# The router's place in the last group of a fused Mamba and mixture-of-experts block, and two queues for its last loads

## The reference, cut to what matters

```python
h = _layernorm(x) * (1 + cb) + sb
out = _swiglu(h, shared_gate_up, shared_down)
logits = einsum('bsd,ed->bse', h, gate_weight)
probs = softmax(logits)
top_p, sel = top_k(probs, 2)
top_p = top_p / (sum(top_p) + 1e-08)
for e in range(8):
    out = out + cw[..., e:e+1] * _swiglu(h, experts_gate_up[e], experts_down[e])
x = x + gb * out
```

## Time and profile before

| what | value |
|---|---|
| median of 3 runs | 744.22 us |
| the profiled execution's own time | 742.37 us |
| its span | 740.6 us |
| mean granted TensorE clock | 0.94 |
| busy PE / DVE / ACT / POOL | 88% / 74% / 59% / 54% |
| last group's shared expert and router | about 362 to 388 us |
| expert tiles | 392 to 715 us |
| end: results, last loads, output | 715 to 740.6 us |

### The profile page before, as it was taken

How to read it: one execution, slowest core, us unless ns; L and a number is a source line. 1 busy time by engine, 2 the same in 40 slices (tenths; PEclk the granted TensorE clock), 3 DMA queues, 4 the chain that set the end, 5 groups by cost and what they waited for, 6 DMA issues and landing times.

```text
span 740.6 us, 12188 instructions
## 1 busy us (share of the span) xinstructions
PE 651.5 (88%) x3026; PEld 501.9 (68%) x3026; DVE 550.7 (74%) x1220; ACT 440.0 (59%) x804; POOL 397.0 (54%) x329
## 2 busy tenths in 40 slices
PE   4778989889998989878778999999999999999960
PEld 1555766667675667656556877877878878777840
DVE  5787988989798997987565776677776667666752
ACT  4647666685767668563444666666666666666640
POOL 2424564738456464826245847567439448472560
PEclk9688989999899999998889999999999999999995
DMA  8303111202112020211331324241320414211407
GB/s 260 78 1 102 50 50 37 64 28 75 39 57 57 29 57 28 82 32 65 108 129 44 114 78 150 66 145 52 122 72 30 157 40 122 99 49 65 135 30 232
DMA packets 47381, 59.83 MB, mean 81 GB/s; under 512 B 8756, under 2 KB 34856, under 8 KB 47360
## 3 DMA queue, kind: packets, MB, share of 16 engines
q1 hardware_dynamic: 41600, 46.91, 20.9%
q0 software_dynamic: 5760, 12.67, 4.9%
HBM read 40.01 MB, written 20.84 MB: 82 GB/s over the span
## 4 chain that ended last, share of the span: by engine, by line
PE 51%; DVE 30%; issue 10%; ACT 2%; DMA 2%; POOL 2%; DVEq 1%; SPq 1%; POOLq 0%; ACTq 0%
PE PS L671 48%; PE PS L674 4%; DVE al L1322 4%; DVE acc L1335 3%; DVE prod L1315 2%; DVE dB L1359 2%; DVE yT L1425 1%; DVE wd L1408 1%; DVE PS L1315 1%; DVE h L1447 1%; DMA yT<-result_dram 1%; DVE stats_a L1299 1%; DVE diag L1412 1%; DVE stats_b L1299 1%; DVE nx_b L1434 1%
## 5 line engine op out<-in xcount | busy, mean ns | idle before, releaser
L1034 ACT ACTIVATE sg<-PS 128x512 f32<-128x512 f32 x216 | 128.7, 597 | 131.9 <-PE PS L671 121.7
L671 PE MATMUL PS<-xh,w_lo 128*128 128x512 f32 x405 | 176.1, 435 | 13.2 <-DVE prod L1315 10.4
L1315 DVE TENSOR_TENSOR PS<-PS,sg 128x512 f32<-128x512 f32 (+1 forms) x160 | 111.3, 697 | 91.7 <-PE PS L671 60.6
L671 PE MATMUL PS<-xl,w_hi 128*128 128x512 f32 x405 | 163.8, 404 | 0.0
L671 PE MATMUL PS<-xh,w_hi 128*128 128x512 f32 x405 | 163.4, 404 | 0.0
L547 POOL DMA_INDIRECT sorted_dram<-h,slot x64 | 73.4, 1147 | 93.0 <-DVE slot L1524 66.9
L671 PEld LDWEIGHTS PS<-xh,w_lo 128*128 128x128 f32 x405 | 78.4, 194 | 46.1 <-DVE prod L1315 16.4
L609 POOL DMA_INDIRECT result_dram<-y_rows,aux_d x84 | 83.0, 989 | 37.5 <-issue 20.1
L1042 ACT CAST ah<-PS 128x512 fp32r<-128x512 f32 (+1 forms) x160 | 93.0, 581 | 15.4 <-DVE PS L1315 13.3
L671 PE MATMUL PS<-ah,w_lo 128*128 128x512 f32 x216 | 93.7, 434 | 8.1 <-ACT ah L1042 4.3
L1322 DVE TENSOR_TENSOR al<-PS,ah 128x512 fp32r<-128x512 f32 x140 | 95.7, 684 | 3.4
(11 more groups left out here) (199 smaller groups left out, 1153.1 us busy)
## 6 DMA issues: line engine op xcount, KB each, us to landing
xin<-sorted_dram SPq DMA_DIRECT2D x20, 516.0 KB
stage<-in_w_gu SPq DMA_DIRECT2D x18, 448.0 KB
sorted_dram<-pad SPq DMA_DIRECT2D x9, 516.0 KB
h<-mods_dram SPq DMA_DIRECT2D x32, 128.0 KB, 6.2
stage<-in_w_dn SPq DMA_DIRECT2D x9, 448.0 KB
tab<-mods_dram SPq DMA_DIRECT2D x8, 384.0 KB, 3.4
out<-X SPq DMA_DIRECT2D x8, 256.0 KB, 5.1
stage<-result_dram SPq DMA_DIRECT2D x6, 256.0 KB, 4.2
```

The source lines that it names most:

```text
L671: return nc.tensor.matmul(out, lhsT, rhs, start=start, stop=stop, **k)
L1034: A.activation(dst, src, ACT.Silu).then_inc(s["silu_done"], 1)
L1315: V.tensor_tensor(product_in(where, c)[0:n, :], bank("up", where, c)[0:n, :], sg[0:n, c % 3, :], ALU.mult).then_inc(s["prod_done"], 1)
```

## The change

It has two parts, in two different stretches.

In the last group: ACT runs `router_exp` ahead of silu 0, where it stood between silu 1 and high 0. DVE runs `weights` and `place` ahead of `product` 0, so that `low` 0 follows `product` 0. PE runs `count_picks` after `gate_up` of chunk 1, where it stood after chunk 2. At the end: SP asks for the even groups' last rows, and ACT, which waits for the same semaphore value, asks for the odd ones.

```diff
-            for g in range(G):
+            for g in range(0, G, 2):
                 sp.dma_start(fin[g], res[1, g]).then_inc(s[f"final_in{g}"], 16)
...
-                if c == 2:
+                if c == 1:
                     count_picks(G - 1, LAST_COUNTS)
...
             copy_h2(G - 1)
+            router_exp(G - 1)
             silu(G - 1, 0, WIDE)
             for c in range(FC):
                 if c + 1 < FC:
                     silu(G - 1, c + 1, WIDE)
-                if c == 0:
-                    router_exp(G - 1)
                 high(G - 1, c, WIDE)
             keep_result(G - 1, WIDE)
...
+            tiles, first = tiles_of(act, E - 1)
+            act.wait_ge(s["results_out"], 64 * (first + tiles + 2))
+            apart(act)
+            rows = result_dram.rearrange("(k g p j) d -> k g p (j d)", k=2, g=G, p=P)
+            for g in range(1, G, 2):
+                act.dma_start(fin[g], rows[1, g]).then_inc(s[f"final_in{g}"], 16)
...
             pick(g)
+            weights(g)
+            place(g, LAST_COUNTS)
             product(g, 0, WIDE)
-            weights(g)
             low(g, 0, WIDE)
-            place(g, LAST_COUNTS)
```

## The result

The changed kernel took 742.42 us (median of 13 runs, 739.87 to 743.5) beside 744.18 us for the kernel before (13 runs). The ratio is 0.9966, with a 95% interval of 0.9952 to 0.9979: faster by 2.5 us, between 1.6 and 3.6. The forecast was 742.6 us and faster. A second set of runs of the same changed kernel gave a ratio of 0.9961 (0.9946 to 0.9976). The profiled execution took 741.35 us, span 739.3.

A forecast was written before the change was run, and what follows sets the result against it. PE was taken to bound the tile stage, DVE's wait for ACT the last group, and full DMA engines the end. Gains of 1.2 and 0.4 us, with zero for the clock, took 744.22 to 742.6 us; range 741.1 to 744.3.

The forecast's parts named there:

- Part one: Last group: DVE's 2.14 us idle goes, product 1 starts earlier; gain 1.2 us, between -0.15 and 1.2.
- The early slots: Last group: slots ready some 3.1 us earlier, for POOL's sorted rows and SP's tile load; costed at nothing.
- The clock: PE's granted clock around its last-group restart: low stretch costs 1.7 us; taken as zero, between -1.7 and 1.7.
- Part two: The end: two queues asking for the last rows fill unfilled DMA stretches; gain 0.4 us, between -0.5 and 0.87.
- The sum: Whole kernel: 1.2 from the last group plus 0.4 from the end, 1.6 us off the median 744.22.
- the second (the clock): PE's restart in the last group: clock stays up or returns sooner, worth up to 1.7 us; chance 0.15.
- The first (the end gains nothing): The end: DMA engines are the limit, so a second queue wins nothing; 743.0 us; chance 0.24.
- third: PE's restart in the last group: the low clock lasts as long again; 744.3 us; chance 0.08.
- fourth: Last group: the counts come no earlier, so DVE waits for PE instead of ACT; 744.0 us; chance 0.04.
- fifth: PE from 374 us on: clock stays low until the shared expert is done; 748.8 us; chance 0.05.

The follow-up runs named there:

- e3: The changed kernel with PE counting the picks behind chunk 2's matmuls again, as before the change; ratio to the kernel before 0.9985.
- e9: The changed kernel with DVE's old order, its plan moved behind low 1, and nine useless PE matmuls in pauses around the first tile; 737.14 us, ratio 0.9914.
- e8: The kernel before with 12 useless matmuls in PE's pause ahead of down 1; the interval of its ratio holds 0.998 and 1.000.
- e11: The changed kernel with ACT's exponential put back behind silu 1, DVE's new order kept; ratio to the kernel before 0.9971.
- e10: The kernel before with nine useless matmuls in PE's three pauses around the first tile; ratio to the kernel before 0.9972.
- e2: The kernel before with only the end's change, SP and ACT each asking for half of the last rows; ratio 0.9995.
- e1: The changed kernel with SP asking for all eight last rows and ACT for none; ratio to the kernel before 0.9967.

## Why the prediction was right, and where it was not

**Part one** was right in each step. The counts begin at 367.01, which is 4.26 us behind `take_logits` (4.32 in the prediction), DVE waits 0.33 for them (0.25 in the prediction) and 0.65 for high 0 (0.7), PE stands 1.71 us ahead of down 0 (1.7). Product 1 is 1.19 us earlier for 1.2, and gated 1.16. e3 shows that this hangs on the counts: with them behind chunk 2 the gain is -0.14 at gated, where the lower bound was -0.15. Two details were off. I put ACT's first table load behind the wait, and it runs ahead of it. It changed nothing here. And ACT was late in the kernel before not because it did two silus, which take 0.6 us each, but mainly because the second of them waited for its gate product until 366.12:

```profile
366.12 0.60 ACT L1034 ACTIVATE sg<-PS 128x512 f32<-128x512 f32 x1 [1.74 <-PE PS L671]
```

The exponential no longer stands behind that wait.

**The early slots** were costed at nothing, and nothing waited for them in the changed kernel. With a start 4.4 us earlier than the kernel before, in e9, PE does wait for the first tile's load.

**The clock** was the weak step, in what it looked at. The prediction took zero, between -1.7 and 1.7, and looked for it only behind PE's restart. There it was right: gated moved by as much as product 1, since the low stretch costs about the same before and after (the 38th matmul at 10.35 and 10.39 us behind the restart). The price of 1.7 us holds as well: at full clock the same matmul comes at 8.8 (e8, e11). But the kernel before has a second low stretch in the first tile, and the changed kernel has none, though PE makes pauses of the same kind there (0.77, 0.83 and 1.14 us). The prediction put nothing for that. Four profiles with a low stretch there have 18.33 to 18.77 us for that tile, the nine without it 16.75 to 17.92, and the means are 1.4 us apart. Against the four at full clock without a late step it is 1.6 to 2.0. e10 isolates it. Why the changed kernel falls on the good side stays open: e2 and e11, 0.14 us apart at gated, fall on different sides. The changed kernel did so in both of its profiles, so it isn't chance from one execution to the next, but nothing in the plan of the change aimed at it.

**Part two** came out larger in the profiles than its bounds: 0.4 us in the sum, between -0.5 and 0.87, and 1.2 us between the means of the spans, or about 1.0 with the 0.2 us lost outside them. Counted from the first issue, the changed kernel moved no more in the first 2.9 us (0.52 MB, and 0.54 before). In the 4.5 us behind them, which hold the two stretches with room, it moved 0.23 MB more, or 0.7 us at 345 GB/s. The rest lies at the very end, which the bound left out: 13.4 us behind the first issue the kernel before still has 0.27 MB to move and takes 2.6 us, and the changed kernel has 0.09 MB and takes 1.6 us. The timed runs cannot decide between 0.4 and 1.0: the end alone gives 0.4 us in e2 (-0.7 to 1.4) and 1.1 in e3 (0.3 to 1.9), and the changed kernel is no more than 0.4 us ahead of e1. ACT's issue, for which I had no row, takes 0.45 us as SP's does. The Trainium skill's rule that issuing from several engines only saves issue time ("DMA: Bandwidth & Descriptors", "Issuing engines are not separate DMA queues") would have given zero in this stretch if the transfers hid all of the issue. The profiles show 1.2, and e3's timing is against zero. The rule that all transfers share the engines agrees with the rows: the share over the 6 us from 732 on is 1.13 before, and 1.14 in the changed kernel with two queues asking.

**The sum.** 1.6 us were forecast. The parts of the mean profiles are 1.2 + 1.4 + 1.2 = 3.8, or 3.6 with the time outside the span, and the timed runs 2.5 (1.6 to 3.6). What takes the rest is not shown. That the forecast median was met to 0.2 us is in part luck: the medians of the two sets differ by 1.8, the ratio says 2.5, and a gain from the clock was missing from the account. The low stretch of the first tile stood in the timeline of the kernel before. Read there, it would have added a term that could win about 1.6 us, though no row said whether it would.

Of the rivals, the second (the clock) came true in another place. The first (the end gains nothing) is against the profiles and e3's timing, but not against e1's and e2's. The third, fourth and fifth did not occur; e3 is the fourth made on purpose.

## What to carry to other kernels

When a part is moved, follow PE's granted clock to the next place where PE restarts after short pauses, also beyond the stretch that is changed: a low stretch can be won or lost there that costs more than the move itself, and which of the two it is can hang on very little (e2 and e11). Put a small step whose result another engine waits for (here the counts) as early in its stream as its own input allows, and test each move of a change by itself: here the reorder of the third engine added nothing. A few matmuls without use in a pause of TensorE can be worth more than the order of the work behind it. And before a difference between two single profiles is given a cause, compare them instruction by instruction: one silu that came 1.2 us late hid most of what the filler in e8 had won.

## What the hardware showed that I had not expected

In all 13 profiles the low stretch that lay over `take_logits` ended 3.3 to 3.5 us behind it, although `take_logits` itself came anywhere from 361.88 to 365.44. Which low stretches follow depends on the kernel and so on PE's work: the kernel before has two, the changed kernel one, e8 and e9 none. In the first tile of the kernel before a low stretch of 3.3 us came with three pauses of PE of 0.77, 0.83 and 1.06 us near each other. Such pauses alone do not decide it, since the changed kernel and e11 have them without a low stretch; but nine matmuls put into them (e10, e9) removed it.

A silu or product began 0.5 to 1.3 us late in some executions, with the same work ahead of it, and PE then stood for it. No profile shows what held it.

ACT's table load ran at 359.73 and ended at 361.01, before the data for the exponential was there at 363.4: a load that has nothing else ahead of it cost nothing while the engine waited. The second load began 0.02 us behind the exponential, at 363.67, and the silu at 364.96, 0.01 us behind the load's end. So a switch of tables took 1.28 us here and no more.
